# Moving the projection of two chunks' values from behind units 3 and 6 to behind units 8 and 11

## What is computed

```python
B, T, C = x.shape                     # 2, 1024, 256; 16 heads of 16, 4 key/value groups
q = (x @ Wq + bq).reshape(B, T, N_HEAD, hd).transpose(0, 2, 1, 3)
k = (x @ Wk + bk).reshape(B, T, N_GROUPS, hd).transpose(0, 2, 1, 3)
v = (x @ Wv + bv).reshape(B, T, N_GROUPS, hd).transpose(0, 2, 1, 3)
q_hat = q / (jnp.linalg.norm(q, axis=-1, keepdims=True) + EPS)
k_hat = k / (jnp.linalg.norm(k, axis=-1, keepdims=True) + EPS)
q_r = apply_rope(q_hat * factor, cos, sin)
k_r = apply_rope(k_hat, cos, sin)
scores = jnp.einsum('bhtd,bhsd->bhts', q_r, k_r) / math.sqrt(hd)
attn = jax.nn.softmax(jnp.where(causal, scores, -jnp.inf), axis=-1)
y = jnp.einsum('bhts,bhsd->bhtd', attn, v)
```

## Time and profile before

| what | before |
| --- | --- |
| median of 3 runs | 801.86 us (801.15 to 804.76) |
| the profiled execution | 804.88 us, its span 803.2 us |
| PE busy | 739.9 us, 92% of the span |
| DVE busy | 411.2 us, 51% |
| ACT busy | 394.7 us, 49% |
| POOL busy | 176.0 us, 22% |
| mean granted clock of PE | 0.957 |
| head() | from 7.2 us (first matmul) to 92.6 us (first matmul of the attention) |

### The profile page before, as it was taken

One profiled execution on the slowest core, in us unless ns is written; L12 is line 12 of the kernel. 1 busy time (PEld: TensorE's weight loads), 2 busy tenths in 40 slices (PEclk: granted clock), 3 DMA queues, 4 the chain that ended last, 5 costly groups with the idle time before them and its releaser, 6 DMA issues.

```text
span 803.2 us, 10943 instructions
## 1 busy us (share of the span) xinstructions
PE 739.9 (92%) x3831; PEld 332.4 (41%) x3831; DVE 411.2 (51%) x998; ACT 394.7 (49%) x517; POOL 176.0 (22%) x186
## 2 busy tenths in 40 slices
PE   4999699999989889797999999989999999999996
PEld 1546322223323535342222222324466457447355
DVE  1578435334768788965133333365432842642524
ACT  1244588887778152553888888773121121131110
POOL 0002424443232223335143222231200200000000
PEclk9996599999999799999899999999999999999998
DMA  8400433332220000022444455470000000000000
GB/s 281 113 0 12 73 56 59 54 55 38 39 41 2 1 0 14 0 38 51 78 81 81 81 83 82 83 194 1 0 1 0 28 0 1 26 0 0 26 1 27
DMA packets 31493, 36.16 MB, mean 45 GB/s; under 512 B 7652, under 2 KB 19745, under 8 KB 31281
## 3 DMA queue, kind: packets, MB, share of 16 engines
q1 hardware_dynamic: 31433, 35.40, 21.7%
HBM read 12.54 MB, written 2.10 MB: 18 GB/s over the span
## 4 chain that ended last, share of the span: by engine, by line
PE 65%; DVE 13%; SPq 9%; ACT 6%; issue 4%; DMA 2%; POOL 1%; DVEq 0%; ACTq 0%; POOLq 0%
PE ps L2034 16%; PE ps L1247 13%; PE ps L1230 11%; PE ps L2058 9%; SPq L967 4%; ACT probs L1311 3%; PE ps L1612 3%; SPq L974 3%; PE ps L398 2%; PE ps L645 2%; PE ps L1599 1%; PE ps L669 1%; DVE stats L289 1%; DVE raw L1147 1%; PE ps L680 1%
## 5 line engine op out<-in xcount | busy, mean ns | idle before, releaser
L1311 ACT ACTIVATE probs<-ps 128x1024 f32<-128x1024 f32 (+1 forms) x320 | 275.8, 967 | 62.6 <-PE ps L1230 62.2
L1230 PE MATMUL ps<-ops_mem 99*128 99x512 bf16 (+3 forms) x768 | 164.0, 335 | 14.2 <-DMA ops_mem<-in_ones 5.5
L1247 PE MATMUL ps<-probs,vstat 128*32 128x512 f32 (+3 forms) x1536 | 166.7, 506 | 10.0 <-DVE raw L1147 7.4
L2034 PE MATMUL ps<-ops_mem,parts_mem 128*128 128x512 f32 x320 | 146.1, 602 | 1.2 <-DVE probs L2086 1.2
L1327 POOL TENSOR_SCALAR_AFFINE_SELECT probs<-probs 128x512 f32<-128x512 f32 x128 | 85.0, 665 | 221.4 <-ACT probs L1311 220.7
L1230 PEld LDWEIGHTS ps<-ops_mem 99*128 99x128 bf16 x768 | 57.4, 99 | 164.0 <-ACT probs L1311 86.4
L1147 DVE COPY raw<-ps 128x512 f32<-128x512 f32 x32 | 22.1, 691 | 149.9 <-PE ps L1247 149.7
L1980 ACT ACTIVATE ops_mem<-ps 128x512 f32<-128x512 f32 x40 | 23.9, 597 | 141.1 <-PE ps L2034 141.1
L2034 PEld LDWEIGHTS ps<-ops_mem,parts_mem 128*128 128x128 f32 x320 | 58.4, 190 | 67.9 <-issue 65.2
L2058 PE MATMUL ps<-parts_mem,probs 128*128 128x256 f32 x320 | 70.5, 380 | 0.0
L2058 PEld LDWEIGHTS ps<-parts_mem,probs 128*128 128x128 f32 x320 | 60.3, 190 | 8.4 <-issue 0.5
(11 more groups left out here) (187 smaller groups left out, 735.2 us busy)
## 6 DMA issues: line engine op xcount, KB each, us to landing
ops_mem<-parts_mem SPq DMA_DIRECT2D x288, 64.0 KB
yT<-in_xT SPq DMA_DIRECT2D x4, 512.0 KB, 8.0
xres<-in_x SPq DMA_DIRECT2D x1, 2048.0 KB, 15.0
ops_mem<-parts_mem SPq DMA_DIRECT2D x48, 32.0 KB
out<-ops_mem SPq DMA_DIRECT2D x3, 512.0 KB, 3.0
rope<-in_rope SPq DMA_DIRECT2D x1, 1024.0 KB, 6.7
parts_mem<-in_wg SPq DMA_DIRECT2D x2, 512.0 KB, 4.9
parts_mem<-in_wu SPq DMA_DIRECT2D x2, 512.0 KB, 6.9
```

The lines of the kernel that those rows point to most:

```text
L1230: last = nc.tensor.matmul(ps[:, bank, o:o + CH - lo], kT[0:KDIM, buf, h if kh == GH else 0, kt * P:(kt + 1) * P], qT[0:KDIM, buf, h, c * C ...
L1247: last = nc.tensor.matmul(ps[32 * h:32 * h + 32, AV, lo:CH], vstat[:, i % 2, kt, h if kh == GH else 0, :], probs[:, s % PRING, h, 0:CH - l ...
L1311: nc.scalar.activation(o, banks, ACT.Exp, scale=score_scale).then_inc(s_exp, 1)
L2034: last = nc.tensor.matmul(ps[:, 4 + 2 * (e % 2) + m, :], w, xT[:, kk, :], start=kk == 0, stop=kk == 1)
```

## The change

`values(0)` is called behind unit 7 and `values(1)` behind unit 10, on PE and on DVE; ORDER is built to match. `decide` and its load stay behind unit 2. Nothing is added or removed, no shape changes.

```diff
+            VALUES_AT = (7, 10)
+
-            ORDER = [(m, n) for m in range(NC) for n in range(NTL + 1) if n < NTL or m < 2] + [(2, NTL), (3, NTL)]
+            ORDER = []
+            for u in range(NU):
+                ORDER.append((u // NTL, u % NTL))
+                if u in VALUES_AT:
+                    ORDER.append((VALUES_AT.index(u), NTL))
+            ORDER += [(2, NTL), (3, NTL)]
...
@@ tensor
-                    if u < 2 * NTL and u % NTL == NTL - 1:
-                        values(u // NTL)
+                    if u in VALUES_AT:
+                        values(VALUES_AT.index(u))
...
@@ vector
-                    if u < 2 * NTL and u % NTL == NTL - 1:
-                        if u < NTL:
-                            loaded(dve, "head")
-                            decide(dve)
-                        values(u // NTL)
+                    if u == NTL - 1:
+                        loaded(dve, "head")
+                        decide(dve)
+                    if u in VALUES_AT:
+                        values(VALUES_AT.index(u))
```

## The result

The changed kernel is slower by about half a per cent. In the first comparison its median is 808.23 us (6 executions, 803.48 to 810.27) against 803.92 us of before (6 executions, 801.15 to 805.42), ratio 1.0053, 95% interval 1.0027 to 1.0079. Two more comparisons gave 1.0062 (1.0034 to 1.0091) and 1.0056 (1.0035 to 1.0076). Over the 24 executions of it in the three comparisons and the 80 of before that ran beside all later experiments the means are 807.9 and 803.5 us: +4.4 +-0.9 us. Four executions in a slower state are left out everywhere (before at 823 and 1208 us, the changed kernel at 1065, the first block alone at 950).

What follows compares the result with a forecast made beforehand. The head's PE and DVE chain to the attention hand-overs was taken as the bound. Terms -0.6, +1.98, +0.03, +0.6, +0.6, +0.68, less 0.30 gave +2.99; 801.86 + 3.0 = 804.9 us, range 802.6 to 808.1.

Steps and rivals of the forecast that it cites:

- The base: Whole kernel before the change: time taken as 801.86 us, the median of the runs shown, to which +3.0 was added.
- The granted clock: TensorE's clock at the head and attention start: no difference taken, +-1.5 us kept for the range.
- Part 1: Front of head(): taking out two value blocks, 1.81 us each, brings unit 7 forward by 3.62 us.
- Part 2: First block behind unit 7: DVE waits for its values, so only 0.6 of the 3.62 us lead remains.
- Part 3: Second block behind unit 10: DVE waits behind turned(10), so factors(2) begins at 65.46 instead of 62.47, +3.0 us.
- Rival (a): PE's lull before factors(1): clock falls there, slowing unit 10's projection; price +2, time 806.9 us; chance 0.23.
- Part 4: Behind factors(2): the +3.0 us passes unchanged through both hand-overs to the end, giving 804.9 us.
- (b): Moved blocks fill PE's gaps and DVE doesn't wait: 801.3 us, or 798.9 if both waits vanish; chance 0.04.
- (c): Hand-over to attention: the delay is absorbed, attention's first items being bound by something else; 801.9 us; chance 0.06.

Runs made afterwards that it cites:

- first block alone: Against the kernel before, only values(0) moved, behind unit 7; values(1) stayed behind unit 5. Ratio 1.0048 (1.0027 to 1.0068), +3.0 +-1.0 us.
- the delay: Kernel before with nothing moved, five extra awaited DVE multiplications behind turned(10). Ratio 1.0034 (1.0009 to 1.0059), +3.4 +-1.5 us.
- rear reads: Changed kernel with DVE's values additions moved to the end of rounds 7 and 10, behind the factors. Ratio 0.9981 (0.9958 to 1.0005) against before.
- fifth profile of the changed kernel: Changed kernel profiled again, unchanged; no lower clock in the head before 68. Sync queue 57.58 us after turned(2), against 55.41 and 55.18 before.
- second block alone: Against the kernel before, only values(1) moved, behind unit 10; values(0) stayed behind unit 2. Ratio 1.0019 (0.9999 to 1.0039), +1.3 +-1.2 us.
- reads at the rear in rounds 9 and 11: Changed kernel with VALUES_AT = (9, 11) and DVE reading both blocks at its round's end, behind the factors. Ratios 0.9966 and 0.9975 against before.

## Why the prediction was wrong

The measured median, 808.23, lies 0.1 us above the range's end of 808.1, and 3.3 above the forecast of 804.9. Two terms of its sum failed. The base was 801.86 and measured 803.5 to 803.9. The granted clock was put at no difference ("nothing in the rows favours one side"), and the changed kernel's mean clock is 0.0061 lower, which goes with 2.2 us. The forecast of the change itself, +3.0, came out as +4.4: +2.3 by the schedule, where 3.0 was forecast, and about +2.2 with the clock, where nothing was. By its own steps:

- **The base.** 2.1 of the 3.3 us are not the change. The forecast stood on 801.86, a median of three executions; with six it was 803.92, and the mean of 80 is 803.5. The range took the base as known, while single executions of before have a standard deviation of 2.1 us.
- **Part 1** held: the block takes 1.81 us at its new place too (42.66 to 44.47), turned(7) is 3.5 to 3.6 us early counted from turned(2) (forecast 3.62) and waits 2.28 (2.27 before).
- **Part 2** held in kind. DVE's wait was 2.52, normalised(0) 0.5 us early (forecast 0.4, counted from turned(7) and the 3.62). What was carried on was more than the 0.6 of the forecast: `turned(10)` in the profile without the fall is 1.2 us early counted from turned(2). The prediction let the lead pass on unchanged because DVE waits for no other engine there. But in both profiles of before DVE stands still for 0.59 us between two of its own operations in factors(1), L855 and L260; in the changed kernel that is 0.15, as elsewhere:

```profile
48.05 0.20 DVE L260 TENSOR_SCALAR small<-small 128x80 int32<-128x80 int32 x1 [0.59 <-DVE small L855]
```

```profile
46.19 0.20 DVE L260 TENSOR_SCALAR small<-small 128x80 int32<-128x80 int32 x1 [0.15 <-DVE small L862]
```

That is 0.4 of the 0.6 by which the lead was larger. The gap is there in every profile in which the reads of both blocks stand ahead of this place in DVE's program (before twice, the delay, the first block alone) and in none in which only one or neither does. Why is not shown.
- **Part 3** held: 3.6 us of wait, and +2.3 us at factors(2) without the fall against +3.0 forecast, the difference being the larger lead and 0.1 in the rows after the wait.
- **Rival (a) happened in most profiles.** It had a chance of 0.23; four of five profiles have the fall at 53 to 55 and neither of before does. Its price was set at +2; in the head it is 1.1 (58.7 against 57.6 at the sync queue). With it the head's loss is 3.4 us, so two errors, the lead and the fall, nearly cancelled; that the head came out near the forecast is luck. The prediction had a row for it (a fall after 1.27 us of waiting) and gave more weight to the one in which the same work with 0.77 had left the clock up. The rule of the Trainium skill that the prediction weighed (page "TensorE: Matmul & The Clock Gate", section "Why this matters for your kernels") would have left the shorter waits harmless; here the measurement decides, since the clock fell around a wait of 1.4 us, and with rear reads after one of 0.5. But its length alone does not decide either: no fall came around 1.39 us in the fifth profile of the changed kernel, nor around 1.82 with the first block alone.
- **Part 4** held for the schedule: +2.9 us at the ninth copy (162.6 on average of five against 159.7 of two), and rivals (b) and (c) are out, (b) by the two waits in the rows, (c) by the delay experiment. Behind 180 us +4.4 in total leaves 1.5 +-0.9 more, which wasn't forecast. From the ninth copy to the end the same instructions took 619.0 to 624.7 us in the five profiles of the changed kernel and 622.8 and 619.6 in those of before.

How much of the total goes with the clock can be estimated from the list of executions: a fit of the time by kernel and mean granted clock over all of them gives 0.36 us for each 0.001, and +2.2 +-0.6 us for the changed kernel at equal clock, near the +2.3 of the head without the fall; its mean clock is 0.0061 lower, which is the other 2.2. For the first block alone the same fit gives +1.7 +-0.8 at equal clock, for the delay +2.2 +-0.8. This is a correlation, and part of the lower clock may be the change's own doing: the fall in the head is in four of its five profiles and in neither of before. A mean lower by 0.0061 is some ten us more at the lower level in an execution (0.0061 of 803 us, times two, as the lower level is half the speed). The profiles, added up in windows of 2 us, have nine: 72.7 us on average in the five of the changed kernel against 63.7 in the two of before. Of these, 5.5 are between 50 and 110 us, that is, in the head and at the start of the attention, and 7.5 between 180 and 500; elsewhere it is 4 less. The part between 180 and 500 is 23.9 to 41.0 us in the five and 20.5 and 27.3 in the two of before, and it is 37.6 with the second block alone and 34.2 and 27.4 with reads at the rear in rounds 9 and 11. So whether the change causes it stays open.

## What to carry to other kernels

An instruction that waits must stand behind everything on its engine that doesn't need the result: here the same move on TensorE lost 4.4 us with the reads ahead of the urgent steps and won 1.9 +-1.4 with the reads behind them, and with the blocks also placed where TensorE had been waiting it won 2.4 +-0.8. When work is taken out of a chain, ask at the new place who will be early, and by how much: an engine that gets there first turns the gain into a wait. And a forecast within half a per cent needs the scatter of the base in its range, not three executions' median.

## What the runs showed of the hardware

TensorE's clock fell not only in waits. With rear reads it fell at 57.4, after PE had waited 0.5 us and had otherwise been at rotation and narrow matmuls; with wide matmuls filled into the wait it stayed up there and fell 5 us later, in the block of 64-column matmuls, while PE was busy for 4.00 of 4.00 us (granted 0.65). So a busy TensorE with little in its matmuls was no protection in these rows. But the same block stood at the upper level in the fifth profile of the changed kernel (58.36, 1.98 us) and in both of rounds 9 and 11 (51.61 in the first, 1.98 us), so it doesn't bring the fall by itself, and what does is not shown. And the mean granted clock of executions of one and the same kernel scatters from 0.942 (807.41 us) to 0.964 (799.32 us) in the kernel before; by the fit that is 8 us, more than the whole effect studied here.
